# The last head of a wide attention layer taken in two halves of its queries, its row sums added by VectorE, the result copied by ScalarE

## What is computed

```python
q, k, v = x @ Wq, ctx @ Wk, ctx @ Wv                 # split into 16 heads of 64
logits  = q @ k.T * 64 ** -0.5
logits[:, token_indices_A] += -20 * (1 - mask_A)      # one bias per query
logits[:, token_indices_B] += -20 * (1 - mask_B)
x = softmax(logits) @ v @ Wo + bo + x
```

## Time and profile before

| | us |
|---|---|
| time, median of 3 runs (lowest, highest) | 4616.84 (4615.51, 4618.89) |
| the profiled execution's own time | 4619.93 |
| its span, first to last instruction | 4618.1 |
| mean granted TensorE clock | 0.987 of full |

### The profile page before, as it was taken

How to read it: one execution, slowest core, us unless ns; L and a number is a source line. 1 busy time by engine, 2 the same in 40 slices (tenths; PEclk the granted TensorE clock), 3 DMA queues, 4 the chain that set the end, 5 groups by cost and what they waited for, 6 DMA issues and landing times.

```text
span 4618.1 us, 56243 instructions
## 1 busy us (share of the span) xinstructions
PE 4523.6 (98%) x20489; PEld 2807.1 (61%) x20489; DVE 2989.6 (65%) x5016; ACT 2262.0 (49%) x4016; POOL 2674.4 (58%) x1281
## 2 busy tenths in 40 slices
PE   8999999999999979999999999999999999999999
PEld 7888865555556545555556555555556655565554
DVE  3321467667766678778746667766767667676766
ACT  3222454454445436666655444444455545454443
POOL 0000367797778611111036887788774877788775
PEclk9999999999999979999999999999999999999999
DMA  4555832221222021011233221222216212222220
GB/s 151 178 188 163 289 79 64 66 68 45 66 64 52 12 39 16 12 15 16 58 109 111 67 67 45 64 68 52 52 46 221 63 39 64 64 68 54 58 48 28
DMA packets 124629, 349.64 MB, mean 76 GB/s; under 512 B 28085, under 2 KB 46005, under 8 KB 113338
## 3 DMA queue, kind: packets, MB, share of 16 engines
q1 hardware_dynamic: 124352, 346.04, 28.4%
HBM read 191.31 MB, written 120.31 MB: 67 GB/s over the span
## 4 chain that ended last, share of the span: by engine, by line
PE 95%; DVE 3%; DMA 1%; issue 1%; SPq 0%; ACT 0%; POOL 0%; DVEq 0%; ACTq 0%
PE ST L957 14%; PE SS L938 13%; PE ST L958 13%; PE OA L968 12%; PE OB L968 11%; PE ST L1090 5%; PE OA L1098 4%; PE SS L1003 4%; PE SS L1076 3%; PE OB L1076 1%; PE SS L977 1%; PE ST L1021 1%; PE ST L1022 1%; PE ST L1023 1%; DVE mpart L1599 1%; PE SS L925 1%
## 5 line engine op out<-in xcount | busy, mean ns | idle before, releaser
L838 POOL TENSOR_TENSOR acc<-acc,P 128x1024 f32<-128x1024 f32 x912 | 2203.2, 2448 | 598.4 <-DVE acc L1526 585.3
L1277 ACT ACTIVATE P<-ST 128x512 f32<-128x512 f32 (+1 forms) x2496 | 1465.4, 598 | 1305.4 <-PE ST L958 1169.8
L1499 DVE TENSOR_REDUCE mpart<-SS 128x1 f32<-128x400 f32 (+1 forms) x3072 | 1627.8, 569 | 676.2 <-PE SS L938 600.4
L938 PE MATMUL SS<-KS,QS 68*128 68x400 f32 (+1 forms) x3072 | 1037.9, 371 | 11.1 <-DMA QS<-stq 8.3
L957 PE MATMUL ST<-QX,KX 128*128 128x512 f32 (+1 forms) x2496 | 1032.9, 414 | 3.6 <-DMA QS<-mrow 2.0
L958 PE MATMUL ST<-QS,KS 69*128 69x512 f32 (+1 forms) x2496 | 989.0, 396 | 0.0
L938 PEld LDWEIGHTS SS<-KS,QS 68*128 68x128 f32 x3072 | 583.9, 190 | 222.6 <-DVE mpart L1499 33.5
L957 PEld LDWEIGHTS ST<-QX,KX 128*128 128x128 f32 (+1 forms) x2496 | 463.0, 185 | 389.2 <-issue 287.6
L968 PE MATMUL OA<-P,Vp 128*64 128x512 f32 (+1 forms) x2496 | 658.3, 606 | 0.0
L968 PE MATMUL OB<-P,Vp 128*64 128x512 f32 (+1 forms) x2496 | 641.3, 592 | 0.0
L1359 ACT ACTIVATE PG<-ST 128x512 f32<-128x512 f32 (+1 forms) x832 | 426.2, 616 | 213.3 <-PE ST L1090 213.0
(11 more groups left out here) (240 smaller groups left out, 4206.4 us busy)
## 6 DMA issues: line engine op xcount, KB each, us to landing
q_parts<-stq SPq DMA_DIRECT2D x96, 512.0 KB, 5.4
QX<-q_parts SPq DMA_DIRECT2D x96, 512.0 KB, 11.3
KX<-k_parts SPq DMA_DIRECT2D x48, 801.0 KB, 9.2
QS<-q_parts SPq DMA_DIRECT2D x45, 512.0 KB
R<-R SPq DMA_DIRECT2D x360, 64.0 KB, 2.0
v_tiles<-sv SPq DMA_DIRECT2D x24, 832.0 KB, 6.4
Vp<-v_tiles SPq DMA_DIRECT2D x24, 832.0 KB, 7.2
k_parts<-skh SPq DMA_DIRECT2D x48, 400.5 KB, 4.9
```

The source lines that it names most:

```text
L838: gp.tensor_tensor(out, out, P[0:k, slot(H, t), q, :], ALU.add).then_inc(pool_a, 1)
L938: pe.matmul(SS[at % 3][:, 0:w], QS[H % 3][0:SROWS, qt * 128:(qt + 1) * 128], KS[H % 3][0:SROWS, o:o + w], start=True, stop=True).then_inc( ...
L1277: act.activation(P[0:k, slot(H, t), j, :], ST[n % 3][0:k, :], ACT.Exp, scale=SCALE).then_inc(act_p, 1)
L1499: dve.tensor_reduce(mpart[H % 2][:, i // len(KCH), c:c + 1], SS[RING_AT["s", H, i] % 3][:, 0:w], AX.X, ALU.max).then_inc(dve_ss, 1)
```

## The change

The 13 × 4 pairs of key tile and query block of a layer's last head are taken in another order: `place` maps the running pair to it, first all 13 key tiles with blocks 0 and 1, then all with blocks 2 and 3. In units of two blocks (m = 0 to 25) the first half ends with m = 12. VectorE adds up this head alone (`last_add`, one instruction of 1024 columns per m), GpSimd none of it; TensorE sums tiles 11 and 12 itself only for blocks 2 and 3 (`OWN`). The sums of the first half are made at the end of step 3 (HALF_STEP). In step 4 ScalarE copies them and OA after the exponentials of that step, and VectorE makes their reciprocals ahead of that step's adds. The second half follows at the end. The final transposes wait block by block for the output adds, and ScalarE copies them. The diff, without the renamed semaphore and the ring's entries:

```diff
+HALF_STEP = STEPS - 4
+def place(h, v, i):
+    if h + 1 < HEADS:
+        return v, i
+    m = 2 * v + i // 2
+    return m % KT, 2 * (m // KT) + i % 2
 def dve_tiles(h):
-    return [1, 2] if h + 1 < HEADS else [1, 2] + list(range(5, KT - 2))
+    return [1, 2] if h + 1 < HEADS else list(range(1, KT))
 def pool_tiles(h):
-    return list(range(3, KT if h + 1 < HEADS else 5))
+    return list(range(3, KT)) if h + 1 < HEADS else []
+OWN = [range(KT, KT), range(KT - 2, KT)]
...
 (TensorE)
-            def last_sums(H):
+            def last_sums(H, c):
+                at = RING_AT["z", H, c]
+                pe.wait_ge(dve_a, adds_before(dve_tiles, H) + last_adds(c * KT + KT - 1))
+                wait_ring(pe, at)
+                for e in range(2):
+                    last = pe.matmul(SS[at % 3][64 * e:64 * e + 64, :], ones[:, 0:64], acc[H % 2][:, 2 * c + e, :],
+                                     start=True, stop=len(OWN[c]) == 0)
+                for t in OWN[c]:
+                    m, k = c * KT + t, rows_of(t)
                     for e in range(2):
+                        last = pe.matmul(SS[at % 3][64 * e:64 * e + 64, :], ones[0:k, 0:64],
+                                         P[0:k, slot(H, m // 2), 2 * (m % 2) + e, :], start=False, stop=t == KT - 1)
+                last.then_inc(pe_z, 1)
...
                     if h + 1 == HEADS and g + 1 == STEPS:
-                        last_sums(H)
+                        last_sums(H, 1)
                     if takes_sums(h, g):
                         sums(H - 1)
+                    if h + 1 == HEADS and g == HALF_STEP:
+                        last_sums(H, 0)
+            def result():
+                for t in range(QT):
+                    pe.wait_ge(dve_ss, DVE_AT["o", BIG * PAIRS - 1, 2 * (t // (QT // JQ)) + 1])
+                    if t >= 3:
+                        pe.wait_ge(act_out, t - 2)
...
 (ScalarE)
-            def take_last_z(H):
+            def take_last(H, c):
                 act.wait_ge(dve_r, z_banks(H))
                 act.wait_ge(d_r, r_spread(H - 1))
-                for c in range(2):
-                    act.wait_ge(pe_z, z_banks(H) + c + 1)
-                    copy(Z2[:, c, :], SS[RING_AT["z", H, c] % 3][:, :]).then_inc(act_z, 1)
+                act.wait_ge(pe_z, z_banks(H) + c + 1)
+                copy(Z2[:, c, :], SS[RING_AT["z", H, c] % 3][:, :]).then_inc(act_z, 1)
+                act.wait_ge(pe_pv, KT * H + (KT if c else KT // 2 + 1))
+                act.wait_ge(pool_on, 4 * H - 2 + 2 * c)
+                copy(Oraw[:, c, :], OAB[c][:, :]).then_inc(act_o, 1)
...
                         if j == 0:
                             exps(H + on, t)
+                    if h + 1 == HEADS and g == HALF_STEP + 1:
+                        take_last(H, 0)
...
+            for t in range(QT):
+                act.wait_ge(pe_out, t + 1)
+                copy(x_out[:, t, :], ST[t % 3][:, 0:C]).then_inc(act_out, 1)
 (VectorE)
+            def last_add(H, m):
+                c, tile, k = m // KT, m % KT, rows_of(m % KT)
+                q = slice(2 * (m % 2), 2 * (m % 2) + 2)
+                out, first = acc[H % 2][0:k, 2 * c:2 * c + 2, :], adds_before(dve_tiles, H)
+                dve.wait_ge(act_p, HU * H + 2 * m + 2)
...
+                else:
+                    dve.wait_ge(dve_a, first + last_adds(m - 1))
+                    dve.tensor_tensor(out, out, P[0:k, slot(H, m // 2), q, :], ALU.add).then_inc(dve_a, 1)
...
                     else:
+                        if g == HALF_STEP + 1:
+                            last_reciprocals(H, 0)
                         for t in PV[g]:
-                            if t in dve_tiles(h):
-                                add(H, t)
+                            for m in (2 * t, 2 * t + 1):
+                                if m % KT > 0 and m % KT not in OWN[m // KT]:
+                                    last_add(H, m)
...
-                for c in range(2):
-                    last_reciprocals(H, c)
+                last_reciprocals(H, 1)
...
-            for t in range(QT):
-                dve.wait_ge(pe_out, t + 1)
-                dve.tensor_copy(x_out[:, t, :], ST[t % 3][:, 0:C]).then_inc(dve_out, 1)
```

More of the change, by code:

```diff
@@ L120, in adds_before @@
 def adds_before(tiles, H):
-    return sum(2 * len(tiles(i % HEADS)) for i in range(H))
+    return sum(2 * len(tiles(i % HEADS)) - (len(OWN[1]) if tiles is dve_tiles and i % HEADS == HEADS - 1 else 0)
+               for i in range(H))
 def group_o_item(h, g, u):
@@ L154, in ring_order @@
                     out.append(("z", first + h - 1, 0))
-        out += [("z", first + HEADS - 1, c) for c in range(2)]
+                if h + 1 == HEADS and g == HALF_STEP:
+                    out.append(("z", first + h, 0))
+        out.append(("z", first + HEADS - 1, 1))
         out += [("o", l * PAIRS + PAIRS - 1, i) for i in range(8)]
@@ L439, in wait_added @@
         def wait_added(eng, H, t):
+            if H % HEADS == HEADS - 1:
+                wait(eng, dve_a, adds_before(dve_tiles, H) + last_adds(2 * t + 1))
+                return
             if t == 0:
@@ L955, in scores @@
                 wait(pe, act_p, n - 2)
+                t, j = place(H % HEADS, t, j)
+                k = rows_of(t)
                 bank, q = ST[n % 3][0:k, :], slice(j * 512, (j + 1) * 512)
@@ L965, in values @@
                     wait(pe, act_o, 2 * H)
[L966 to L969, removed]
+                for i in range(JQ):
+                    tile, j = place(H % HEADS, t, i)
+                    k, r = rows_of(tile), 64 * (j % 2)
+                    last = pe.matmul(OAB[j // 2][r:r + 64, :], Vp[n % 2][0:k, tile, 64 * e:64 * e + 64],
+                                     P[0:k, at, i, :], start=tile == 0, stop=tile == KT - 1)
                 last.then_inc(pe_pv, 1)
@@ L1050, in head @@
                     if h + 1 == HEADS and g + 1 == STEPS:
-                        last_sums(H)
+                        last_sums(H, 1)
                     if takes_sums(h, g):
                         sums(H - 1)
+                    if h + 1 == HEADS and g == HALF_STEP:
+                        last_sums(H, 0)
[4 more added lines that the diff above has]
+                        pe.wait_ge(act_out, t - 2)
+                    for ct in range(CT):
+                        last = pe.transpose(ST[t % 3][:, ct * 128:(ct + 1) * 128], xacc[:, ct, t * 128:(t + 1) * 128],
+                                            ident[:, :])
+                    last.then_inc(pe_out, 1)
             def end(l):
@@ L1057, in end @@
                     output(l * PAIRS + PAIRS - 1, i)
+                if l + 1 == BIG:
+                    result()
             def group_project(rnd, j):
@@ L1170, in _ @@
                     group_layer()
-            pe.wait_ge(dve_ss, DVE_AT["o", BIG * PAIRS - 1, 7])
-            for t in range(QT):
[L1174 to L1179, removed]
         @block.scalar
@@ L1274, in exps @@
                 for j in range(JQ):
-                    n, k = HU * H + JQ * t + j, rows_of(t)
+                    n, k = HU * H + JQ * t + j, rows_of(place(H % HEADS, t, j)[0])
                     act.wait_ge(pe_st, n + 1)
@@ L1526, in add @@
                         dve.tensor_tensor(out, out, P[0:k, slot(H, t), q, :], ALU.add).then_inc(dve_a, 1)
+            def last_add(H, m):
[3 more added lines that the diff above has]
+                dve.wait_ge(act_p, HU * H + 2 * m + 2)
+                if tile == 1:
+                    b = slice(2 * ((m - 1) % 2), 2 * ((m - 1) % 2) + 2)
+                    wait(dve, pe_z, z_banks(H - 1))
+                    dve.tensor_tensor(out, P[:, slot(H, (m - 1) // 2), b, :], P[:, slot(H, m // 2), q, :], ALU.add)\
+                        .then_inc(dve_a, 1)
+                else:
+                    dve.wait_ge(dve_a, first + last_adds(m - 1))
+                    dve.tensor_tensor(out, out, P[0:k, slot(H, m // 2), q, :], ALU.add).then_inc(dve_a, 1)
             def reciprocals(H):
```

28 lines of the change are left out of this document (9 added, 19 removed).

## The result

| | before | changed |
|---|---|---|
| time, median (lowest, highest), us | 4616.84 (4615.51, 4621.6), 7 runs | 4632.53 (4630.13, 4638.67), 7 runs |
| the profiled execution's own time, us | 4619.93 | 4633.1 |
| its span, us | 4618.1 | 4631.3 |

The ratio is 1.0032 with a 95% interval of [1.0021, 1.0044]: the changed kernel is slower by 15.7 us. That is inside the range on record by half a microsecond, on the side of its slower rival, and twice what the sum said. 0.3% is also past the line of 0.2% at which the prediction counts a change: not the outcome with a chance of 0.57 (no change that counts) came, but the one with 0.37 (slower).

What follows compares the result with a forecast made beforehand. TensorE, busy 98% of the span, was taken to bound the kernel. Later ends of the three wide layers, 3.3 + 3.0 + 1.5 = +7.8 us on the median 4616.84, gave 4624.6 us, range 4613 to 4633.

Steps and rivals of the forecast that it cites:

- its slower rival: Rival called "the clock falls a second time", ending on the slow side at 4632.4 us; chance 0.25.
- the sum: Forecast total over the three wide layers' ends: 3.3 + 3.0 + 1.5 = +7.8 us, median 4624.6.
- the second sum: TensorE's ones-matmuls for query blocks 2 and 3, six matmuls, forecast 4.3 to 5.2 us at the low clock.
- the wait removed: TensorE's old 3.01 us stop between the sums and the first output projection in each wide layer's last head.
- the three ends: Last layer's final copies +3.3 us, fourth output add between wide layers +3.0, mean square's reading before the small layer +1.5.
- The wait: TensorE, ready at 4591.9, waits for VectorE's adds before the second sum: 5.7 us, bounds 3.2 and 6.5.
- The chained add: Each VectorE add in the last head waits for the one before: 1.24 us each, between 1.17 and 1.30.
- The clock: TensorE's granted clock falls to 0.50 behind the wait, back 3.4 to 5.9 us after work resumes; 2.1 us per end.
- T: Start of the second sum; the denominators were forecast at T + 5.1, between 4.65 and 5.5 us after it.
- the first fourteen adds: VectorE's adds before the last eight in the last head, forecast as covered, done before TensorE wants them.
- the clock falls a second time: Rival: TensorE stops 2.3 us before output 3 and the low clock returns, 2.6 us per layer; 4632.4 us, chance 0.25.
- VectorE keeps up: Rival: the eight adds are done when TensorE is ready for the second sum; 4601.2 us, chance 0.05.

Runs made afterwards that it cites:

- Experiment 1: Changed kernel with the first half's reciprocal in a layer's last head moved behind all eight adds of the second half; 4606.16 us, ratio to before 0.9978.
- Experiment 3: Changed kernel with ScalarE's copies of the first half's sums and output moved ahead of step 4's exponentials; 4628.26 us, ratio to before 1.0026.
- experiment 4: Changed kernel with six unused matmuls put ahead of TensorE's wait for the second sum in each wide layer; 4622.0 us, ratio to before 1.0009.

## Why the prediction was right, and where it was off

The sign, the mechanism and the place were as written: a wait of TensorE for VectorE ahead of the second sum takes the place of the wait removed, because the first half's reciprocal stands ahead of eight adds. Experiment 1 shows that: with that one line the wait goes, and 26.4 us of the median (26.5 from the first sums to the layers' ends, 31.54, 25.35 and 33.56 us). The size was half of what was measured. The excess over the sum is 7.9 us. 4.4 of it lie in the three ends that the sum was made of: 3.4 because the second sums started later than forecast (1.8, 1.4 and 0.2 us), and 1.2 because the denominators took 0.4 longer in each layer, less 0.1 to 0.2 of small terms. The other 3.5 are outside the mechanism: about 1 at the last stores and between the ends, and 2.5 between the profiled executions and the medians. Three terms are behind the 4.4:

- **The wait.** 5.7 us forecast, 7.34 measured in the last layer (6.69 and 5.81 in the others). In the old times (the head begins 6.38 us later in this execution, by its first output add, 4545.60 for 4539.22) the second sum starts at 4599.36, not 4597.6. 1.4 of the 1.8 are the reciprocal's start: "the copy" was to release it at 4582.4, "just after the divides". The divides were later than the copy, since the spreading took 7.8 us there and not 6.6, and head 14's reciprocal ended 0.8 later. Two conditions within 0.6 us of each other should have been carried as a range, not as one. In the first layer the copy was the releaser, by 0.02 us, the second sum started 0.2 later than forecast, and the wait was 5.81. Experiment 3 confirms the divides as what holds the reciprocal. The range was also too narrow: the recorded terms at their upper ends (eight adds at 1.30 and 2.6 for the divides) add up to 6.8 us of waiting, not 6.5, and the last layer is above both.
- **The chained add.** Taken at 1.24 us; eight took 12.23, of which the pair beside the divides had 2.21 a piece and the others 1.33 (from one start to the next in the chain of waits: 4599.14, 4600.47). That is 0.4 more than forecast for the eight with their divides, and 1.33 lies above my bound of 1.30. With 1.17 the eight would have been 9.4 + 1.8 = 11.2 us, too little. The Trainium skill (VectorE: DVE Perf Modes, The DRAIN you can't avoid) gives that a semaphore after each operation costs nothing extra, measured on copies. No run here has adds without a semaphore. Those of the kernel before signal one each too and come at 1.17; what is new is that each waits for the one directly ahead of it, and a sentence on signalling gives no price for that. For the port, two divides cost 2 × 0.88 us, as the 1.9 taken from rows; the 2.5 by the Trainium skill's rule (SBUF — State Buffer, Who interferes with whom), a whole instruction each, is too much here.
- **The clock.** Its level was right (0.50 behind the stop) and so was its share, 6.0 us in the traces of experiment 4 against the 6.3 on record (2.1 at each end). That it came back 3.4 to 5.9 us after work resumed was too short for the first two layers, 9.1 and 9.4, but the longer spell fell on outputs 0 to 2, behind which output 3 had to wait in any case. The denominators came at T + 5.5 in all three layers, where I had taken 5.1 and 5.5 as the bound.

Held: first sum 1.0 us instead of 0.9; the first fourteen adds covered; the last add 9.9 us after the denominators (4621.10 − 4611.23 = 9.87); end of the copies 4.8 after it. The three ends (last, middle, first layer) gave, against the old ones and from the same head's beginning, +5.5, +4.6 and +2.2 us where 3.3, 3.0 and 1.5 were forecast; 12.2 of the profiled pair's 13.2 us are there, and 1.3 in the last store's landing (5.4 us behind the copies instead of 4.1), with smaller differences of both signs between. The median moved by 2.5 us more than the profiled executions; those single executions spread by 8 us.

Of the rivals, "the clock falls a second time" gave 4632.4 and the measured time is 4632.5, but not by that mechanism: TensorE stopped for 1.94 us between outputs 2 and 3 in the last layer, and its outputs then came at the full clock (ten instructions in 4.56 us), and the other two layers had no such stop at all. So the second fall did not happen in the profiled execution, which is all that can be read, and that the time lies inside the range, which was widened for it, and so near this rival's figure, is luck in part. That a stop of 1.94 us can cost the clock is so nevertheless: the first layer of experiments 1 and 4 and the second of experiment 3 show it. "VectorE keeps up" is what experiment 1 made: 4601.2 was worked out, 4606.16 measured. 1.7 of the 5 us between are the first layer's last ten output instructions, 6.26 us instead of 4.56 behind the stop of 1.94; the rest lies within what two medians can tell. I had given this rival 0.05 for good reason: nothing but another order of the queue brings it about.

## What to carry to other kernels

When half of a reduction is finished early, its epilogue must not stand ahead of the other half's ready work in an in-order queue: list for each of its waits what is queued behind, and place it where the work behind it isn't needed first. An idle VectorE just before a late VectorE is the sign for it. Where TensorE must wait, read the granted clock behind the wait as well: here it was about half of the loss (6.0 of the 12.2 us by which the three ends came later).

## What the runs showed of the hardware

- Matmuls that nobody reads, put into TensorE's waits of 6 to 7 us, made the kernel 7 to 10 us faster (7.3 in the traces, 6.0 of them behind the waits, and 10.5 in the medians).
- A stop of 2.70 us was followed by 3.4 us at 0.50, with TensorE busy all the while. A stop of 2.07 us, 15 us later, left the clock at 1.00 (both in experiment 3, second wide layer). A stop of 1.94 us was followed by a low clock in one layer of three and by the full clock in the other two (experiment 1). Behind stops of 5.81, 6.69 and 7.34 us the clock stayed at 0.50 for 9.1, 9.4 and 5.2 us of work (changed kernel).
- A VectorE add of 1024 columns that waits for the one directly before it comes every 1.33 us; two that needn't take 2.35. Beside a GpSimd divide it comes every 2.21.
- The four final stores of 512 KB took 3.0 to 5.2 us each to land, differently from execution to execution, whichever engine had made the copies.
